# First graph layer of a two-layer graph network: gather normalised rows, sum by node and relation, apply the relation weights once a batch

## The reference

```
msg = layernorm(x)[src] * edge_weight             # one row of 256 for each edge
agg[r, v] = sum of msg over the edges u->v of relation r      # r = 0..7
out[v] = sum over r of blockdiag(agg[r, v], W[r]) # 8 blocks of 32x32 for each relation
x1 = x + out                                      # then layernorm(x1) feeds the first experts
```

## Time and profile before

| | |
|---|---|
| times of three runs | 5299.99, 5288.77, 5298.8 us |
| profiled execution | 5290.91 us, of which the span from first to last instruction is 5289.2 us |
| busy share of the span | PE 87%, weight loads 60%, DVE 43%, ACT 14%, POOL 60% |
| mean granted TensorE clock | 0.789 of 2.4 GHz |
| chain that ended last | POOL's gathers at L1414 28% of the span, "issue" 10% |

### The profile page before, as it was taken

One profiled execution on the slowest core, in us unless ns is written; L12 is line 12 of the kernel. 1 busy time (PEld: TensorE's weight loads), 2 busy tenths in 40 slices (PEclk: granted clock), 3 DMA queues, 4 the chain that ended last, 5 costly groups with the idle time before them and its releaser, 6 DMA issues. The chain is left out here.

```text
span 5289.2 us, 61603 instructions
## 1 busy us (share of the span) xinstructions
PE 4579.8 (87%) x16124; PEld 3170.3 (60%) x16124; DVE 2292.5 (43%) x7526; ACT 729.9 (14%) x1757; POOL 3175.5 (60%) x3360
## 2 busy tenths in 40 slices
PE   3879998899998998973788857999999999999998
PEld 1347776677766776752555524666666666666665
DVE  5655555555555555555344422333333332333322
ACT  0310000000000000003233300111111111111112
POOL 0147777777777777761000057777777777777760
PEclk8975555555555555555899968999999999999999
DMA  5753333333333333332111144444444444444430
GB/s 112 260 170 104 105 104 104 105 105 105 105 104 104 105 105 105 105 96 81 46 38 44 37 137 118 119 122 127 123 122 117 125 125 126 122 118 123 125 104 9
DMA packets 303625, 569.96 MB, mean 108 GB/s; under 512 B 71688, under 2 KB 196510, under 8 KB 303579
## 3 DMA queue, kind: packets, MB, share of 16 engines
q0 software_dynamic: 159648, 442.73, 30.2%
q1 hardware_dynamic: 119913, 104.30, 6.2%
q10 hardware_dynamic: 24018, 22.39, 1.6%
HBM read 476.61 MB, written 92.57 MB: 108 GB/s over the span
## 5 line engine op out<-in xcount | busy, mean ns | idle before, releaser
L668 PE MATMUL win<-onehot,ring 128*128 128x128 f32 x6448 | 1836.9, 441 | 195.1 <-DMA ring<-table,index 147.0
L1414 POOL DMA_INDIRECT ring<-table,index x1616 | 1556.8, 963 | 547.3 <-issue 492.0
L649 POOL DMA_INDIRECT ring<-table,index x1612 | 1530.5, 949 | 512.0 <-issue 490.8
L668 PEld LDWEIGHTS win<-onehot,ring 128*128 128x128 f32 x6448 | 1417.3, 307 | 615.3 <-DMA ring<-table,index 454.3
L707 DVE TENSOR_TENSOR acc<-acc,win 128x256 f32 x1612 | 680.5, 422 | 804.5 <-PE win L668 639.8
L1576 PE MATMUL bank<-ring,acc 128*128 128x264 f32 x3232 | 877.0, 408 | 135.6 <-DMA ring<-table,index 129.7
L1576 PEld LDWEIGHTS bank<-ring,acc 128*128 128x128 f32 x3232 | 594.6, 194 | 441.2 <-DMA ring<-table,index 259.6
L1754 DVE TENSOR_SCALAR acc<-iota,off 128x128 f32<-128x128 f32 x1734 | 355.2, 296 | 633.4 <-ACT off L1427 630.5
L685 DVE TENSOR_SCALAR onehot<-iota,scal 128x128 f32<-128x128 f32 x1612 | 459.1, 356 | 116.5 <-issue 108.8
L1592 PE MATMUL bank<-acc,wa 128*128 (+1 forms) x832 | 378.5, 598 | 26.5 <-ACT ework L1462 26.5
L1617 PE MATMUL bank<-wo,ework 128*128 128x256 f32 x1664 | 381.8, 383 | 1.8 <-DVE y L1825 1.8
(11 more groups left out here) (256 smaller groups left out, 2396.7 us busy)
## 6 DMA issues: line engine op xcount, KB each, us to landing
ring<-table,index POOLq DMA_INDIRECT x3228, 2.8
table<-rrows SPq DMA_DIRECT2D x49, 1024.0 KB, 4.2
sums<-acc ACTq DMA_DIRECT2D x101, 132.0 KB
acc<-sums ACTq DMA_DIRECT2D x13, 528.0 KB
y<-x SPq DMA_DIRECT2D x13, 512.0 KB, 4.1
table<-frow SPq DMA_DIRECT2D x48, 132.0 KB, 1.7
rx<-in_x POOLq DMA_DIRECT2D x48, 128.0 KB, 2.8
nx<-in_x POOLq DMA_DIRECT2D x48, 128.0 KB, 2.5
```

What stands on the lines that cost most here:

```text
L649: pool.indirect_dma_start(ring[par * BT + t][:], None, k.table0_d, bass.IndirectOffsetOnAxis(ap=index[par][:, t:t + 1], axis=0)).then_inc( ...
L668: ins = pe.matmul(win[t % (2 * QUAD)][:, h, :], ring[par * BT + t][:, h * P:(h + 1) * P], onehot[t % (2 * QUAD)][:], start=True, stop=True)
L1414: pool.indirect_dma_start(ring[:, par * BT + t, :], None, k.table1_d, bass.IndirectOffsetOnAxis(ap=index[par][:, t:t + 1], axis=0)).then_i ...
```

## The change

- The table is gone. `edge_tables` also loads x in five chunks of 1.28 MB on ACT's queue (125 partitions with 50 nodes each), takes statistics on DVE, normalises on ACT and stores the result, 6.4 MB, to `xn_d`. The statistics stand between the copies of the turned arrays in DVE's list. The scattered writes of `ends_d`, `both_d` and `starts_d` are issued later than before.
- `gnn0` takes the place of `relation_table`, `gnn0_edges` and `gnn0_nodes`. It gathers rows of `xn_d` by source node, four times 16 tiles of ring. The one-hot has 64 columns: 8 relations times the 8 nodes from the tile's first node on (`NEAR`). DVE adds the 128x128 result to `cells`, which hold a batch's sums by relation and node (136 node columns). Once a batch PE applies the weights (`weigh`: 16 matmuls of 128 columns), and adds what the batch before left over through one matmul of 256 columns with `carry_hot`; ACT stores the 128-node window to `sums0_d` and clears the cells.
- Node work (`norm`, `turn`, `place`) runs for 128 nodes every second batch, in the same loop.
- `narrow` is 1 when each tile spans fewer than 8 nodes, each batch fewer than 128, and the batches come in time for the node rounds; otherwise a slower `general` path runs. In these inputs, counted from the destinations, the widest tile spans 5 further nodes, the widest batch 66, and the tightest round has 22 nodes in hand.

```diff
@@ edge_tables, ACT
-            act.wait_ge(ready, 1)
+            for c in range(CHUNKS_X):
+                act.dma_start(x[:, chunk(c), :], by_parts(g["x"])[:, chunk(c), :]).then_inc(xloads[c], 16)
+            load_tables(act, k, ACT.Sqrt)
...
+            act.wait_ge(ready, 3)
             act.dma_start(k.starts_d.rearrange("(k q) e -> q k e", q=P), starts[:]).then_inc(k.starts_stored, 16)
@@ edge_tables, DVE
+            spread(0)
+            for i, held in enumerate((off_t[:], k.src[:], rel_t[:], k.meta[:, WEIGHT_KIND, :])):
                 for b in range(0, BLOCKS, 4):
...
+                scale(i)
+                spread(i + 1)
+            scale(CHUNKS_X - 1)
@@ gnn0, POOL
+            def gather(b, m, tiles, first=False):
+                pool.wait_ge(indexed, b + 1)
+                for t in range(tiles):
+                    if t % QUAD == 0 and not first:
+                        pool.wait_ge(summed, QUADS * b - 4 * QUADS + t // QUAD + 1)
+                    past_waits(pool, k)
+                    pool.indirect_dma_start(ring[:, m * BT + t, :], None, k.xn_d,
+                                            bass.IndirectOffsetOnAxis(ap=index[m][:, t:t + 1], axis=0)
+                                            ).then_inc(got[m * QUADS + t // QUAD], 16)
@@ gnn0, ACT
+            def period(b, m, n, j, p, mine, prev, gathers, window):
...
+                if window:
+                    move_window(b - 1, (m - 1) % 2)
+                if gathers and later:
+                    stage_index(b + 3, (m + 3) % 4)
+                if window:
+                    act.copy(cells[(m - 1) % 4], zero[:].unsqueeze(1).broadcast_to([P, H * RELS, P + NEAR])
+                             ).then_inc(cleared, 1)
+                    keep_window(b - 1, (m - 1) % 2)
@@ gnn0, PE
+            def quad(b, m, n, q):
+                pe.wait_ge(hot, QUADS * b + q + 1)
+                if not (isinstance(b, int) and b == 0):
+                    pe.wait_ge(added, QUADS * b - QUADS + q + 1)
+                pe.wait_ge(got[m * QUADS + q], 16 * QUAD * (n + 1))
+                for t in range(QUAD):
+                    for h in range(H):
+                        ins = pe.matmul(win[q][:, t, h * CELLS:(h + 1) * CELLS],
+                                        ring[:, m * BT + q * QUAD + t, h * P:(h + 1) * P],
+                                        onehot[:, q * QUAD + t, :], start=True, stop=True)
+                ins.then_inc(summed, 1)
+
+            def weigh(b, m):
...
+                    pe.matmul(rows_ps, carry_hot[:, m % 2, :], nodes[:, (m - 1) % 2, :], start=True, stop=False,
+                              skip_group_check=True)
+                for h in range(H):
+                    for r in range(RELS):
+                        ins = pe.matmul(rows_ps[:, h * P:(h + 1) * P], cells[m][:, h * RELS + r, 0:P],
+                                        k.wblk[:, h, r, :], start=(first and h == 0 and r == 0),
+                                        stop=(r == RELS - 1), skip_group_check=True)
...
+            def period(b, m, n, j, p, mine, prev, gathers, window):
+                for q in range(QUADS):
+                    if gathers and q < quads_of(b):
+                        quad(b, m, n, q)
+                    if q == 2 and window:
+                        weigh(b - 1, (m - 1) % 4)
+                for j2, r in parts0(j, p, mine, prev):
+                    if r == STEP0:
+                        turn(j2)
@@ gnn0, DVE
+                    for q in range(QUADS):
+                        if q < quads:
+                            add(b, m, q, bases)
+                        if not (isinstance(b, int) and b == BATCHES - 1) and q < quads_of(b + 1):
+                            one_hots(b + 1, (m + 1) % 4, q)
+                for j2, r in parts0(j, p, mine, prev):
+                    if r == 1:
+                        norm(j2, 1 - m // 2, n if m else n - 1)
@@ ffn0
-                        rhs = k.acc[:, h, cols(gi * GCOLS, n)]
+                        rhs = k.acc[:, h, cols(gi * GCOLS + AHEAD0, n)]
```

More of the change, by code:

```diff
@@ L65 @@
 ROUNDS = GROUPS
+STEP0 = 2
+ROUNDS0 = NODE_TILES - 1
+FIRST0 = N - ROUNDS0 * P
+AHEAD0 = P - FIRST0
+NEAR = 8
+CELLS = NEAR * RELS
+ROWS_X = 50
+PARTS_X = N // ROWS_X
+CHUNKS_X = 5
+CHUNK_X = ROWS_X // CHUNKS_X
 CARRY = BT
@@ L350, in _ @@
+            for c in range(CHUNKS_X):
+                normalise(c)
+            act.wait_ge(ready, 3)
             act.dma_start(k.starts_d.rearrange("(k q) e -> q k e", q=P), starts[:]).then_inc(k.starts_stored, 16)
@@ new lines, in parts0, with batch_fours, either_path @@
+def parts0(j, p, mine, prev):
+    return [(j - 1, p + STEP0)] * prev + [(j, p)] * mine
+def batch_fours(eng, emit):
+    with eng.Fori(0, BATCHES // 4) as i:
+        for m in range(4):
+            emit(4 * i + m, m, i, BT)
+    emit(BATCHES - 1, 0, BATCHES // 4, LAST_TILES)
+def either_path(nc, k, eng, narrow, general):
+    _, flag = nc.values_load_multi_w_load_instructions(k.narrow[:], engines=[eng.engine], min_val=0, max_val=1)
+    with eng.If(flag[0] == 1):
+        narrow()
+    with eng.Else():
+        general()
@@ new lines, in add @@
+            def add(b, m, q, bases):
+                dve.wait_ge(summed, QUADS * b + q + 1)
+                if q == 0 and not (isinstance(b, int) and b < 4):
+                    dve.wait_ge(cleared, b - 3)
+                for u in range(QUAD):
+                    if u:
+                        dve.wait_ge(chain, (QUAD - 1) * (QUADS * b + q) + u)
+                    elif q or not (isinstance(b, int) and b == 0):
+                        dve.wait_ge(added, QUADS * b + q)
+                    here = cells[m][:, :, cols(bases[q * QUAD + u], NEAR)]
+                    dve.tensor_tensor(here, here, win[q][:, u, :].rearrange("p (c n) -> p c n", n=NEAR), ALU.add
+                                      ).then_inc(added if u == QUAD - 1 else chain, 1)
@@ new lines, in period @@
+            def period(b, m, n, j, p, mine, prev, gathers, window):
+                if gathers:
+                    quads = quads_of(b)
+                    _, bases = nc.values_load_multi_w_load_instructions(
+                        k.base[0:1, cols(b * BT, quads * QUAD)], engines=[dve.engine], min_val=0, max_val=P,
+                        skip_runtime_bounds_check_because="edge_tables clamps every step to 0..P")
+                    if not (isinstance(b, int) and b == 0):
+                        carry(b, m)
+                    for q in range(QUADS):
[3 more added lines that the diff above has]
+                            one_hots(b + 1, (m + 1) % 4, q)
+                for j2, r in parts0(j, p, mine, prev):
+                    if r == 1:
+                        norm(j2, 1 - m // 2, n if m else n - 1)
@@ L820, in route @@
+            either_path(nc, k, dve, narrow, general)
 def route(nc, k, g):
```

767 lines of the change are left out of this document (386 added, 381 removed).

## The result

| | before | changed |
|---|---|---|
| median | 5295.24 us (4 runs) | 5007.85 us (4 runs, 5006.13 to 5010.35) |
| ratio | | 0.9458, 95% interval 0.9442 to 0.9475 |
| profiled execution | 5290.91 us | 5006.31 us |
| mean granted TensorE clock | 0.789 | 0.858 |

The forecast was 4961, so 47 us too low; the time lies inside the range (4925 to 5080), at the upper edge of the case's own range (4937 to 5010).

A forecast was written before the change was run, and what follows sets the result against it. POOL's issue of 1612 gathers at 1.254 us each bounds the gather stage, with 399.0 us outside the gathers removable. Terms -218 + 5 - 125 = -338 on 5290.9 give 4953, plus 7.9 to the median: 4961 us, range 4925 to 5080.

The forecast's parts named there:

- the case's own range: Total time if the main forecast case holds, from the terms' bounds: 4937 to 5010 us; chance 78%.
- The front: Everything ahead of the first gather: it starts at about 108 us instead of 326, -218 us; bounds 98 and 128.
- The gathers: gnn0's 1612 gathers: POOL still paces at 1.254 us each, DVE's changed work adds 5 us (0 to 22).
- PE in a batch: Gather stage: PE needs 23 us at the lower clock, 16 with the clock rising behind weigh, below POOL's 20.06.
- PE paces the gathers: Rival, gather stage: if the clock never rises, 297 us more, 5258; a part of it, 5010 to 5100; chance 12%.
- DVE in a batch: Gather stage: DVE's work sums to 13.7 of 20.06 us, adds 0.39 and one-hots 0.20 each, hidden under POOL.
- the slower rival: DVE paces the gathers through the strided add; at 1.1 us an add the total is 5470 us; chance 4%.
- Behind the last gather: From the last gather to `route`: 34 us instead of 158.6, -125 us; bounds 26 and 46.
- DVE in the front: Ahead of the first gather: DVE's casts, statistics, copies and offsets sum to 66.9 us, ending at 101.
- Loads: Start of the front: 9.7 MB at 242 GB/s by 44 us; edge arrays land between 25 and 44, taken as 34.
- Scattered writes: Front: three tables issued at 82 us take 23, done at 105, just behind DVE; bounds 95 and 120.
- the front is not hidden: Rival: x, statistics and scattered writes run in turn, first gather at 160, total 5013 us and up; chance 5%.

The follow-up runs named there:

- e1: Changed kernel with the loads of x in pieces of 112 and 13 partitions instead of 125; 6368 us in one run, changed kernel 6376 on that chip.
- e5: Changed kernel, x loads and stores in 112 and 13 partitions, later x pieces behind edge arrays, pads, weights and scattered tables reordered; 6342 us against 6376 (median of four).
- e2: Changed kernel with both the loads of x and the stores of normalised rows in pieces of 112 and 13 partitions; 6362 us in one run, changed kernel 6376.
- e6: Like e5, but SP's row stores reordered around the scattered tables and gathers of 512 B, not 1 KB; 4941.8 us against 5294.5 for the kernel before.

## Why the prediction was right, and the step that failed

The gain comes from where the prediction said: 399 us of stages in which no gather ran are gone, what takes their place mostly runs beside other work, and the gathers kept their pace. That the time lies inside the case's own range is in part luck. The front alone, 61.8 us late and far outside its own bounds (98 and 128), would have put it at 5023, above the 5010. The gathers (6 under their term), the second graph stage (2.9) and the median, which stood 1.5 us above the profiled execution and not 7.9, gave some 15 us back.

- **The gathers** (+5, measured -1.0). Right, and for its reason: POOL paces with 1.253 us a gather, half the bytes change it by 0.3%. The new DVE work cost POOL nothing, so the 48 us that the prediction had worked out and set aside did not come; whether these DVE instructions ran in a two-port mode at all, no row shows.
- **PE in a batch.** Estimated 16 us at a mean clock of about 0.7; measured 1604.6/101 = 15.9 at 0.72. A weight load beside 64 columns was forecast at 0.21 to 0.22 at the lower level and 0.107 at the upper. The timeline of one batch:

```profile
1190.58 3.49 PEld L756 LDWEIGHTS bank<-spare,ring 128*128 128x128 f32 x16 [3.90 <-issue]
...
1199.37 3.65 PEld L756 LDWEIGHTS bank<-spare,ring 128*128 128x128 f32 x32
```

  3.49/16 = 0.218 and 3.65/32 = 0.114. So 64 columns cost as much as 128. And the clock rises with weigh, already while it runs, in both batches looked at. In the first it stayed up for three stretches of 3.4 us and fell behind one with 1.97 of 3.40 busy, in the second for two. Over the whole stage the trace has 99 times at the upper level for 101 batches, 829 us together, 8.4 us each; before there were 32. So the rival "PE paces the gathers" is answered by the clock and not by the columns. The stretches of the first batch:

```profile
1193.60:1197.00 3.40, 3.40 (x16) 3.22 (x16) 2.05 (x8) 0.00 (x0) 2.49 (x4) 0.52 0.33 102
1197.00:1200.40 3.40, 3.40 (x33) 3.40 (x32) 0.00 (x0) 0.72 (x3) 2.61 (x3) 1.00 0.37 116
1200.40:1203.80 3.40, 2.77 (x25) 2.63 (x24) 1.90 (x8) 2.39 (x7) 2.67 (x3) 1.00 0.48 141
1203.80:1207.20 3.40, 1.97 (x16) 1.86 (x16) 2.54 (x15) 0.00 (x0) 2.49 (x4) 0.99 0.33 96
1207.20:1210.60 3.40, 0.91 (x5) 0.94 (x5) 1.35 (x7) 0.00 (x0) 2.49 (x4) 0.50 0.46 136
```

- **DVE in a batch.** The forecast counted an instruction from one start to the next, as the earlier trace rows give it. By that count an add takes 1.55/4 = 0.39 us, as forecast, and a one-hot 0.98/4 = 0.25 and not 0.20, which with the forecast's other terms makes the batch about 14.4 us (an estimate) and not 13.7:

```profile
1194.40 1.55 DVE L855 TENSOR_TENSOR spare<-spare,bank 128x128 f32 x4 [4.59 <-PE bank L756]
1195.86 0.98 DVE L835 TENSOR_SCALAR spare<-iota,scal 128x64 f32<-128x64 f32 x4
```

  DVE's busy time is 1036/101 = 10.3 us a batch, and was 11.0 before. The strided add has no price of its own, and the slower rival was far off.
- **Behind the last gather** (-125, measured -124.3). 30.9 us to `route` where 34 were forecast, with the same steps: two weighs, the window, the last round of `norm`, `turn` and `place`. The stages from there to the second graph took 3.4 us longer than before (578.0 and 574.6), which stands in no term (the shift in `ffn0` was put at nothing). That -124.3 is so near to -125 is two small errors that cancel.
- **DVE in the front.** 66.9 us forecast, 67.1 measured.
- **Loads: the step that failed.** "If the two queues share evenly, the edge arrays land between 25 (no harm) and 44; I take 34." They landed at 74.5, 40.5 us later. The rate was taken from transfers over 128 partitions; x has 125, and was carried by 5 of 16 engines. That is 23.1 us of the miss: with all engines and the same order the casts begin at 51.4 (e1). The other 17.4 us are the even sharing, which did not come, and the thirteen small loads behind the large ones, which were in no term: the large loads were in at 44 only, and the small ones took 7 more. So the upper bound of 44 would have failed on all engines too. Only another order of the queues brings the casts under 34 (28.9 in e5). And 242 GB/s was not the best rate of the trace, but the highest mean of a stage: the edge loads of before ran at 307 to 311 between 9 and 19 us.
- **Scattered writes: the five engines once more.** "so 105; bounds 95 and 120", 4 us behind DVE. They were held behind the stores of the rows on the same five engines, and the first gather stood 28.3 us behind DVE instead of 7 (21.3 us). 40.5 + 21.3 are the 61.8 us by which the front missed. With loads and stores on all engines the first gather stands 6.8 us behind DVE, as forecast, but at 125.0 (e2), still 17 us late, by the rest of the loads. The 106.45 of e6 is near the forecast's 108, but with another order of the queues and by other terms: casts at 29.4 and not 34, and 10.1 us behind DVE and not 7.
- The rival "the front is not hidden" (5%, 5013 and up) describes the first gather (169.9) better than the forecast's own case does; the loads came in turn with the rest, the statistics were overlapped. It should have had a real chance, since no row of before shows a transfer of x with 125 partitions.
- All of this is true of the first chip. That the sign turns on another one was in no rival.

## What to carry to other kernels

Look at the partition count of each large transfer before its size: with 125 partitions it got 5 DMA engines here, and what another queue had spread over all 16 waited for those five; the sign in the profile was a DMA share of 0.31 at a steady rate. Cutting it into 112 and 13 gave 45 us (170.5 to 125.0), and ordering the queues by what is needed first some 14 to 19 more. And where one engine's work for each gather paces a loop, fewer bytes or columns elsewhere buy next to nothing (0.3% for half the bytes), while more instructions on PE can be free on one chip and cost the whole gain on another.

## What the runs showed that I had not expected

- Transfers of 125 partitions ran at 130 GB/s on both chips, in pieces of 112 and 13, with the edge arrays beside them, at 236 GB/s on the second one.
- An indirect gather of 128 rows costs POOL 949 ns with 1 KB a row and 945 ns with 512 B.
- Two speeds: the kernel before takes 5295 us on one chip and 6156 to 6248 on another. On that one, PE and DVE start their instructions 0.7 us or a multiple apart in phases beside POOL's gathers, and the denser kernel loses more by it (816 us against 381 in the gather stage).
